# Planner order, key tiles and store queue of a fused attention and recurrence kernel

## What is computed

```
qkv = x @ c_attn_w + c_attn_b
k, v = image row and 512 word rows;  scores = q k^T / sqrt(32), causal
x = x + softmax(scores) v @ c_proj_w + c_proj_b
h_t = tanh(h_(t-1) @ Wh + x_t @ Wx + b),  h_(-1) = cond
out_t = x_t + h_t
```

## Time and profile before

| | us |
|---|---|
| median of 3 runs (1730.48 to 1731.11) | 1730.66 |
| the profiled execution | 1726.08 |
| its span, first to last instruction | 1724.3 |
| PE busy, PEld busy | 1526.2, 1291.9 |
| DVE busy, ACT busy, POOL busy | 821.8, 716.3, 383.1 |

### The profile page before, as it was taken

The page is one execution under the profiler, slowest core; times in us unless marked ns, Lnnn a source line. Parts: engine busy times, 40 slices in busy tenths (PEclk is TensorE's granted clock), DMA queues, the critical chain, the costliest instruction groups (busy, mean ns, idle before and its releaser), DMA issues.

```text
span 1724.3 us, 65681 instructions
## 1 busy us (share of the span) xinstructions
PE 1526.2 (89%) x28397; PEld 1291.9 (75%) x28397; DVE 821.8 (48%) x2596; ACT 716.3 (42%) x2285; POOL 383.1 (22%) x552
## 2 busy tenths in 40 slices
PE   5788888989999899999999999999999999777775
PEld 4677776878778777878788887888888888666664
DVE  5355454445444445545555555555555556222221
ACT  2345444434444344544444454544544446111111
POOL 0634342313122031312313131220311210000000
PEclk8888898999999999999999999999999999999999
DMA  7455445424434344535444455654555544000000
GB/s 250 167 155 172 134 154 167 122 79 137 119 102 128 85 145 126 152 113 149 131 120 137 110 154 148 161 155 113 148 140 137 139 127 103 8 15 9 15 9 14
DMA packets 135247, 204.72 MB, mean 119 GB/s; under 512 B 19880, under 2 KB 85672, under 8 KB 134448
## 3 DMA queue, kind: packets, MB, share of 16 engines
q1 hardware_dynamic: 107120, 125.50, 27.9%
q0 software_dynamic: 27840, 75.02, 12.9%
HBM read 133.06 MB, written 67.37 MB: 116 GB/s over the span
## 4 chain that ended last, share of the span: by engine, by line
PE 75%; DMA 7%; DVE 6%; issue 5%; ACT 5%; SPq 1%; POOL 1%; DVEq 0%; ACTq 0%; POOLq 0%
PE rec L915 23%; PE turned L851 8%; PE dense L421 7%; PE dense L422 6%; PE dense L423 6%; PE rec L908 6%; PE scores L843 4%; PE scores L915 4%; PE pv L864 3%; DVE pre L763 3%; DMA xin<-x 3%; DMA kq<-kq_dram 3%; ACT states L617 3%; PE pv L882 2%; DVE probs L712 1%
## 5 line engine op out<-in xcount | busy, mean ns | idle before, releaser
L915 PE MATMUL rec<-wh,states 128*32 128x128 f32 x14336 | 484.2, 276 | 67.3 <-ACT states L617 65.6
L915 PEld LDWEIGHTS rec<-wh,states 128*32 128x32 f32 x14336 | 375.4, 110 | 133.9 <-ACT states L617 101.3
L575 ACT ACTIVATE probs<-probs,nmax 128x128 f32<-128x128 f32 (+3 forms) x512 | 287.1, 561 | 194.7 <-DVE nmax L712 186.5
L617 ACT ACTIVATE states<-pre 128x32 f32<-128x32 f32 x512 | 133.2, 260 | 473.9 <-DVE pre L763 473.2
L712 DVE CUSTOM_DVE_ANT_0 probs<-scores,msk,nimg 128x128 f32<-128x128 f32 (+3 forms) x512 | 275.5, 545 | 58.0 <-PE scores L843 52.7
L763 DVE STREAM_TRANSPOSE pre<-rec 128x128 f32<-128x128 f32 x448 | 141.7, 316 | 334.6 <-PE rec L915 330.7
L851 PE MATMUL turned<-ident,probs 128*128 128x128 f32 x1280 | 240.8, 288 | 21.7 <-ACT probs L575 17.9
L843 PE MATMUL scores<-kq 96*128 96x128 f32 (+3 forms) x512 | 203.3, 402 | 19.7 <-DMA kq<-kq_dram 18.1
L851 PEld LDWEIGHTS turned<-ident,probs 128*128 128x128 f32 x1280 | 145.3, 141 | 79.5 <-issue 47.5
L516 POOL DMA_DIRECT2D kq_dram<-qs_hi x128 | 92.5, 725 | 319.7 <-DVE qs_lo L685 305.5
L721 DVE COPY probsT<-turned 128x128 f32<-128x128 f32 (+3 forms) x256 | 125.1, 489 | 67.6 <-PE turned L851 63.3
(11 more groups left out here) (153 smaller groups left out, 2246.0 us busy)
## 6 DMA issues: line engine op xcount, KB each, us to landing
kq<-kq_dram SPq DMA_DIRECT2D x96, 320.0 KB, 5.2
kq<-kq_dram SPq DMA_DIRECT2D x96, 256.0 KB, 4.5
kq<-kq_dram SPq DMA_DIRECT2D x96, 192.0 KB, 3.6
kq_dram<-qs_hi POOLq DMA_DIRECT2D x128, 128.0 KB, 2.7
kq_dram<-ks_hi POOLq DMA_DIRECT2D x128, 128.0 KB, 3.1
kq<-kq_dram SPq DMA_DIRECT2D x96, 128.0 KB, 2.9
xin<-x SPq DMA_DIRECT2D x32, 256.0 KB, 3.9
kq_dram<-qs_lo POOLq DMA_DIRECT2D x64, 128.0 KB, 3.4
```

The source lines that it names most:

```text
L575: act.activation(probs[:, g % PROBS, 0:n], probs[:, g % PROBS, 0:n], ACT.Exp, scale=-1.0, bias=nmax[:, e, h:h + 1], accum_out=rowsum[:, e, ...
L617: act.activation(state_cells(g), pre[:].rearrange("p f (b z) -> p f b z", z=GROUP)[:, :, :, s], ACT.Tanh).then_inc(h_ready, 1)
L915: last = pe.matmul(rec_bank(g // GROUP)[Q * j:Q * j + Q, 0:P], state_tile(g - 1)[:, f, :], wh[:, f, P * j:P * j + P], start=False, stop=f ...
```

## The change

Five things are changed.

1. `order`: each quarter of a block (from one trip's first proj to the next, the first from "finished") gets its 32 steps evenly by planned cost, so no deadline is left to force a row.
2. `values`: each v product is two events of 6 matmuls, `vfirst` and `v`, in the same bank; only the second counts as ready.
3. `main_order`: `side` is dealt by planned cost; an event is emitted when the cost due per remaining unit exceeds half of its own, events of cost 0 at once. In the last trip the projs are dealt up to h 16.
4. Key and query tiles have the size of their block in one room of 5120 elements a partition: 5 tiles in block 0, 3 in block 1, 2 in blocks 2 and 3. A load waits for the last group that used any of its space.
5. The q and k stores are issued by SP with the same lag, 1.3, instead of POOL.

By the new rule the projs come at h 11, 13, 15 and 17. xload, both xsplits and "finished" have cost 0 and follow the last proj at once, at h 17. Then q0 comes at h 19, k0 at 21, q1 at 23, k1 at 25, q2 at 28, k2 at 30, and the last image score at 31; in the first half vfirst at h 0, v at 1, q3 at 2, k3 at 4, the second v at 7 and 9.

The diff is cut: left out are the counting of banks, the number of the semaphores of the tiles, and the places where PE waits for them.

```diff
@@ -30,7 +30,8 @@
 PROBS = 4
 TURNED = 6
-TILES = 2
+ROOM = 2 * HC * (P + S)
 VTILES = 3
 TURN_LAG = 4
 PV_LAG = 10
...
@@ -50,20 +51,41 @@
             "total": 0.5, "norm": 0.2, "attnlow": 0.9, "proj": 0.2, "step": 0.1, "hist": 0.8},
     "ACT": {"xsplit": 0.0, "q": 0.2, "k": 0.2, "score": 0.8, "turn": 0.2, "imgprob": 0.2, "imgturn": 0.2,
             "rowturn": 0.2, "norm": 0.6, "step": 0.5, "out": 0.2},
-    "POOL": {"mskload": 0.9, "mskscale": 1.0, "vstore": 1.0, "out": 1.0, "q": 1.3, "k": 1.3},
-    "SP": {"xload": 0.8, "vimgload": 0.9, "kqload": 1.4, "vload": 0.5},
+    "POOL": {"mskload": 0.9, "mskscale": 1.0, "vstore": 1.0, "out": 1.0},
+    "SP": {"xload": 0.8, "vimgload": 0.9, "q": 1.3, "k": 1.3, "kqload": 1.4, "vload": 0.5},
 }
-DENSE_KINDS = ("q", "k", "v", "imgscore", "imgturn", "rowturn", "proj", "out")
+DENSE_KINDS = ("vfirst", "q", "k", "v", "imgscore", "imgturn", "rowturn", "proj", "out")
 def block_of(g):
     return g // PAIRS
+def tile_places():
+    places, counts = [], [0] * (ROOM // (HC * 2 * P))
+    for group in range(GROUPS):
+        first = group // (8 * PAIRS) * 8 * PAIRS
+        size = HC * P * (block_of(group // 8) + 2)
+        n = (group - first) % (ROOM // size)
+        over = [m + 1 for m, (_, _, _, at, width) in enumerate(places)
+                if at < n * size + size and n * size < at + width]
+        counts[n] += 1
+        places.append((max(over, default=0), n, counts[n], n * size, size))
+    for n in range(len(counts)):
+        mine = [m for m, place in enumerate(places) if place[1] == n]
+        assert all(places[b][0] > a for a, b in zip(mine, mine[1:]))
+    return places
+PLACES = tile_places()
 def main_order():
-    out, seen, loads = [], set(), [("kqload", group, 0, 0.0) for group in range(TILES)]
+    out, seen, loads = [], set(), [("kqload", group, 0, 0.0) for group in range(GROUPS) if not PLACES[group][0]]
     loads += [("vload", group, 0, 0.0) for group in range(VTILES)]
     def emit(events):
...
@@ -81,7 +103,7 @@
         return [("q", g, c, 1.5), ("k", g, c, 1.5), ("imgscore", g, c, 0.5)]
     def values(g, e):
-        return [("v", g, e, 2.7), ("vstore", g, e, 0.0)]
+        return [("vfirst", g, e, 1.45), ("v", g, e, 1.45), ("vstore", g, e, 0.0)]
     def begin(g):
         return [("xsplit", g, k, 0.0) for k in range(2)]
...
@@ -100,7 +122,7 @@
             side, until = values(g, 0) + chunk(g, 3) + values(g, 1), 9
         if h == 10:
-            side, until = [], UNITS - 1
+            side, until = [], UNITS - 1 if g + 1 < TRIPS else H
             if 0 < g <= TRIPS:
                 side += finish(g - 1)
             if g + 1 < TRIPS:
...
@@ -125,17 +147,19 @@
             v = u - TURN_LAG
             emit([("turn", v, 0, 0.05 + 0.11 * (block_of(v // UNITS) + 1))])
         if u < HEADS:
-            if u % HC == HC - 1 and u // HC + TILES < GROUPS:
-                loads.append(("kqload", u // HC + TILES, 0, 0.0))
+            if u % HC == HC - 1:
+                loads += [("kqload", group, 0, 0.0) for group in range(GROUPS) if PLACES[group][0] == u // HC + 1]
             emit([("score", u, 0, max(0.11, 0.053 * (block_of(g) + 1)) + 0.1)])
             if h2 == 15 and block + 2 < 2 * TRIPS:
                 emit([("mskload", (block + 2) // 2, block % 2, 0.0)])
         if 0 < block <= 2 * TRIPS:
             emit({1: [("imgprob", block - 1, 0, 0.0)], 2: [("total", block - 1, 0, 0.0)],
                   4: [("imgturn", block - 1, 0, 0.15)], 5: [("rowturn", block - 1, 0, 0.5)]}.get(h2, []))
-        take = len(side) if g >= TRIPS or h >= until else -(-len(side) // (until + 1 - h))
-        emit(side[:take])
-        side = side[take:]
+        share = sum(w for *_, w in side) / max(until + 1 - h, 1)
+        while side and (g >= TRIPS or h >= until or side[0][3] == 0.0 or share > side[0][3] / 2):
+            share -= side[0][3]
+            emit([side.pop(0)])
     return out
...
@@ -146,17 +170,18 @@
     ends = {g: n for n, (kind, g, i, _) in enumerate(main) if kind == "finished"}
     place = {}
     for b in range(BLOCKS - 1):
-        first, last = ends[(b + 1) * PAIRS - 1] + 1, begins[(b + 2) * PAIRS - 1]
-        whole = sum(w for *_, w in main[first:last])
-        done, n = 0.0, 0
-        for at in range(first, last):
-            done += main[at][3]
-            while n < P and (done >= whole * (n + 0.5) / P
-                             or at + 1 == begins.get((b + 1) * PAIRS + n // STEPS)):
-                place.setdefault(at, []).append(b * P + n)
-                n += 1
-        assert n == P
+        first = ends[(b + 1) * PAIRS - 1] + 1
+        for n in range(PAIRS):
+            last = begins[(b + 1) * PAIRS + n]
+            whole = sum(w for *_, w in main[first:last])
+            done, t = 0.0, 0
+            for at in range(first, last):
+                done += main[at][3]
+                while t < STEPS and (done >= whole * (t + 0.5) / STEPS or at + 1 == last):
+                    place.setdefault(at, []).append(b * P + n * STEPS + t)
+                    t += 1
+            first = last
     plan = {name: [] for name in ("PE", "DVE", "ACT", "POOL", "SP")}
     clock = 0.0
...
@@ -237,7 +263,7 @@
         qs_lo = sb("qs_lo", [P, 2, 2 * P], F32R)
         ks_hi = sb("ks_hi", [P, 2, 2 * P], F32R)
         ks_lo = sb("ks_lo", [P, 2, 2 * P], F32R)
-        kq_tiles = sb("kq", [P, TILES, HC * (P + S)], F32R)
+        kq_tiles = sb("kq", [P, ROOM], F32R)
         vbuf = sb("vbuf", [P, 2 * D + VTILES * BLOCKS * P])
         msk = sb("msk", [P, 2, S])
...
@@ -385,8 +411,8 @@
             eng.wait_ge(dense_copied[n], before + 1)
         def heads_tile(group):
-            n = P + P * (block_of(group // 8) + 1)
-            return kq_tiles[:, group % TILES, 0:HC * n].rearrange("p (j n) -> p j n", j=HC)
+            _, _, _, at, size = PLACES[group]
+            return kq_tiles[:, at:at + size].rearrange("p (j n) -> p j n", j=HC)
         def rec_bank(k):
...
@@ -457,18 +483,30 @@
+                elif kind in ("q", "k"):
+                    wait_copied(sp, kind, g, i)
+                    if kind == "q":
+                        parts, at, stored = (qs_hi, qs_hi, qs_lo), 0, q_stored
+                    else:
+                        parts, at, stored = (ks_hi, ks_lo, ks_hi), P * (p + 1), k_stored
+                    for part, src in enumerate(parts):
+                        sp.dma_start(kq_dram[part, r, :, i, :, at:at + P],
+                                     src[:, i % 2, :].bitcast(F32).rearrange("p (e t) -> p e t", e=2)
+                                     ).then_inc(stored[i % 2], 16)
                 elif kind == "kqload":
                     trip, k = divmod(g, 8)
                     p, r = divmod(trip, PAIRS)
                     e, c = divmod(k, C)
                     sp.wait_ge(q_stored[c % 2], 48 * (2 * trip + c // 2 + 1))
                     sp.wait_ge(k_stored[c % 2], 48 * (2 * trip + c // 2 + 1))
-                    if g >= TILES:
-                        sp.wait_ge(scores_ready, HC * (g - TILES + 1))
+                    after, n, *_ = PLACES[g]
+                    if after:
+                        sp.wait_ge(scores_ready, HC * after)
                     for part in range(3):
                         sp.dma_start(heads_tile(g)[Q * part:Q * part + Q].bitcast(F32),
                                      kq_dram[part, r, :, c, e, 0:P + P * (p + 1)]
-                                     .rearrange("(j d) t -> d j t", d=Q)).then_inc(tile_loaded[g % TILES], 16)
+                                     .rearrange("(j d) t -> d j t", d=Q)).then_inc(tile_loaded[n], 16)
                 elif kind == "vload":
                     trip, k = divmod(g, 8)
                     p, r = divmod(trip, PAIRS)
...
@@ -505,17 +543,6 @@
-                elif kind in ("q", "k"):
-                    wait_copied(pool, kind, g, i)
-                    if kind == "q":
...
@@ -815,13 +845,14 @@
                         last = split_product(d[:, 0:2 * P], wqkv_hi[:, f, w0:w0 + P], wqkv_lo[:, f, w0:w0 + P],
                                              xT_hi[:, f, :], xT_lo[:, f, :], f == 0, f == C - 1)
                     last.then_inc(dense_ready, 1)
-                elif kind == "v":
+                elif kind in ("vfirst", "v"):
                     mine = slice(P * i, P * i + P)
-                    for f in range(C):
-                        last = split_product(d[:, :], xT_hi[:, f, mine], xT_lo[:, f, mine],
+                    for f in range(C // 2) if kind == "vfirst" else range(C // 2, C):
+                        last = split_product(bank("v", g, i)[:, :], xT_hi[:, f, mine], xT_lo[:, f, mine],
                                              wqkv_hi[:, f, 2 * D:3 * D], wqkv_lo[:, f, 2 * D:3 * D],
                                              f == 0, f == C - 1)
-                    last.then_inc(dense_ready, 1)
+                    if kind == "v":
+                        last.then_inc(dense_ready, 1)
```

(29 more changed lines are left out.)

## The result

The changed kernel takes 1765.35 us, the kernel before 1730.88 us in the same comparison: ratio 1.0192, interval 1.0165 to 1.0219. The forecast was 1722 us and its range ended at 1745. The profiled execution took 1764.68 us; its span, 1762.9 us, is 38.6 us longer than before.

The account below looks back on a forecast made before the run. PE bounds the kernel, with some 120 us of waits winnable by reordering. Terms -17 - 14 - 16 - 3.5 + 28 + 13 + 1 + 0 = -8.5 us on 1726.1 give 1717.6; the median's 4.6 us makes 1722, range 1690 to 1745.

Parts of the forecast that it names:

- the tile room: Dealing by time and five tiles: -16 us in block 0; tile waits at trip ends of blocks 1 and 2: -3.5 us.
- the tile was loaded long before: Block 0's trip ends: dense work stands at h 28 to 31 and the tile is already loaded; 20 of 22 us won.
- the forecast's own signs of being wrong: PEld's waits at h 17 to 19 under 2 us, step waits above 60 us in blocks 1 to 3, tile loads longest.
- The stores on SP: 384 q and k store issues leave POOL, where they were idle cover, for SP: 0 us (bounds -3, +6).
- The estimate of 9 us for k3's way: Block 0: k3's splits, stores, loads and landings take some 9 us, where PE has about 8 us of work.
- The input load and the clock: h 17 to 19, trips 1 to 14: PE waits behind ACT's casts, +28 us; low clock after such waits, +13 us.
- The rival in which the clock falls at every load: Clock falls at all fourteen input loads: 9 us more, 1731 us; chance 0.05, inside the forecast case.
- Steps by quarters: Rows of steps in blocks 1 to 3 go, 24 us, with 7 us given back: -17 us (bounds -24, -5).
- v in halves: 24 v products in blocks 1 to 3: one step mostly falls between halves, -14 us (bounds -24, 0).
- The third rival: Steps find no better cover: half the waits of parts 1 and 2 move to other units, 1738 us; chance 0.13.
- the room's two terms: -16 us for dealing and five tiles in block 0, -3.5 us for trip-end tile waits in blocks 1 and 2.
- the forecast's others: Steps by quarters -17, v in halves -14, input load +28, clock +13, small terms +1, stores by SP 0 us.

Follow-up runs that it names:

- e12: The kernel before with only the room of 5, 3, 2 and 2 tiles: 1753.12 us, ratio 1.0113.
- e16: The kernel before with only the room, the first tile of a block at a place long free: 1719.93 us, ratio 0.9932.
- e1: The changed kernel with the first tile of each block at a place long free: 1728.26 us, ratio 1.0012 to the kernel before.
- e2: The changed kernel with two tiles of the full size at fixed places: 1709.8 us, ratio 0.99 to the kernel before.
- e11: The kernel before with only the q and k stores moved to SP's list: 1738.21 us, ratio 1.0037.
- e3: The changed kernel with the q and k stores issued by POOL again: 1751.99 us, ratio 1.0145 to the kernel before.
- e7: The changed kernel with early projs, stores on POOL and each block's first tile at a place long free: 1675.46 us, ratio 0.968 to the kernel before.
- e15: The changed kernel with early projs and each block's first tile at a place long free: 1688.62 us, ratio 0.9761 to the kernel before.
- e4: The changed kernel with projs, input load and splits dealt one a unit from h 10: 1727.76 us, ratio 0.9987 to the kernel before.
- e8: The kernel before with only the steps spread by quarters: 1705.11 us, ratio 0.9856.
- e9: The kernel before with only v split into two events: 1722.8 us, ratio 0.9934.
- e10: The kernel before with only side dealt by planned cost: 1753.3 us, ratio 1.011.

## Why the prediction was wrong

**The step that failed is the tile room**, "-16 us (bounds -24, -5)" with "-3.5 us (-4.1, 0)". The forecast worked out when k and q are stored and when a tile is needed. It took "the tile was loaded long before" from the number of places and never asked whose place the first tile of a block lies on. Alone the part costs 20 us instead of gaining; moving the first places turns this into a gain of 12 (e12, e16). In the changed kernel the places are worth 31 to 37 us (e1). No rival named this. Two of the forecast's own signs of being wrong did appear: tile loads are the longest waits, and the waits of steps in blocks 1 to 3 are 60.5 us. The gain of 16 us that the forecast put at block 0's trip ends did not need five tiles, either: in the profiled execution of e2, with two, block 0 is 15 us shorter than before.

**The stores on SP**, "0 (bounds -3 ... +6)", cost 6 us alone, at the bound (e11), but 13 by the medians, 8 by the ratios, within the change (e3), and 13 between e7 and e15. The term counted issue times and what stands behind a store, but not that a load right behind a store makes SP wait for its landing, with the next store behind. The estimate of 9 us for k3's way was of the right size, had SP been on time; in trip 1 DVE had k3's low part ready at 106.5 and its store went out at 113.2, 7 us later. By the page cited there (the Trainium skill, DMA: Bandwidth & Descriptors, Issuing engines are not separate DMA queues) only the time to initiate is at stake; the runs show more, the order within the issuer's list.

**The input load and the clock**, +28 and +13, were right: 41 forecast, 38 measured by undoing (e4) and 40 by the same edit on e1 (e15), at the place and with the neighbours named. The waits were put somewhat too long: 4.0 us in trip 9 instead of 5.3, since the chain took 5.6 us and not 6.4; in the eleven trips together 43 us instead of 51. The rival in which the clock falls at every load does not hold: it is low behind seven of these eleven.

**Steps by quarters**, -17, measured -25 (e8). **v in halves**, -14, measured -11 (e9). Both mechanisms hold; the first was undersized because I gave back 7 us that did not return. The third rival, that the waits only move, is refuted.

The five parts alone sum to -25 - 11 + 19 + 6 + 20 = +9 us; together they cost 34. The 25 us between lie where the parts meet, and the traces say in part where. Little of it is at the tiles: the three boundary waits are 33.5 us in the changed kernel and 28.5 in e12, and block 0's tile waits, 34.1, are less than the 38 that e10, e11 and e12 alone add up to. Most is at the tanh and the bias in blocks 1 to 3: by e8, e9 and e10 alone these waits would be 48 us, and they are 73. Late projs add 10.5 us to them alone (e10) and 26 in the changed kernel (e4). Why they cost more beside the other parts was not taken apart.

Without the room's two terms the forecast's others sum to -8.5 + 19.5 = +11. e2, the changed kernel with two tiles, lies 17 to 20 us under before, and it would be wrong to read this as an error of 30 us in those terms. By the stages, 8 of it stand before the first score, for which no term was written, and 15 in block 0, which the forecast had credited to dealing and tiles together (-16). After block 0, where the other terms belong, e2 is 7 us longer than before, against their +11. So the rest was forecast about rightly, as far as single executions tell, and the miss of 43 us is the room's: from e2 to the changed kernel it is 51 to 56 us, where the forecast had gains.

## What to carry to other kernels

When a buffer is cut into places of a new size, write down for the first user of the new cut whose last use it overlaps, and start the new cut at the place that falls free first. In a queue that works strictly in order, count a dependent transfer right behind its own source's store as a stall of the whole queue, and look at what stands behind it. Events of no planned cost are not free: a load and the casts behind it need distance, whatever they cost themselves.

## What was not expected of the hardware

Several tiles fetched together took longer to land than such DMAs do in the median. In e12, at the end of trip 3, SP issues nine DMAs of 192 KB in 4.2 us and PE goes on 3.3 us after the last; they take 4.7 us (median) from issue to landing, against 3.6 for all DMAs of that size in the run. At the end of trip 7 six DMAs of 256 KB are issued in 3.5 us, PE goes on 6.7 us after the last, and they take 8.4 us, against 4.5. Meanwhile the DMA engines are busy 0.94 of the time at the first place (the last three figures are PE's clock, the DMA share and GB/s):

```profile
257.50:265.00 7.50, 0.01 (x1) 0.01 (x1) 0.00 (x0) 0.00 (x0) 0.00 (x0) 0.50 0.94 218
```

In block 0 the mean granted clock was 0.86 of 2.4 GHz in e1, where eight waits for tiles sum to 35.0 us and the longest is 9.0, and 0.94 in e2, where sixteen sum to 18.5 and none is over 3.8. Block 0 is 23 us shorter in e2, between its first score and that of block 1. Some 13 of it is less wait for tiles, and PE is busy 162 us in it instead of 169, which fits the higher clock. In this pair many short waits were cheaper than a few long ones by more than their sum.
